# A new order of PE's, ACT's and POOL's instructions in the three-stage front of a decoder block

## The reference, cut to what matters

```python
x = _layernorm(x + _L0_attn_ref(x), axis=-1)          # dilated attention, 16 heads, segments of 64, step 2
x = _layernorm(x + _L0_xattn_ref(x, ctx_512, L0_xattn_Wq, L0_xattn_Wkv_expand, L0_xattn_Wout), axis=-1)
x = _layernorm(x + _L0_ffn_ref(x, L0_ffn_gate_w, L0_ffn_w_gate, L0_ffn_w_up, L0_ffn_w_down), axis=-1)
...
# dilated attention: every head attends, inside a segment, over its 32 rows; q = k = v = x
scores = jnp.einsum('bnhqd,bnhkd->bnhqk', g, g) * scale
out = jnp.einsum('bnhqk,bnhkd->bnhqd', jax.nn.softmax(scores, axis=-1), g)
...
# cross attention: 16 heads of 16 columns, 128 x 128 causal scores per head, keys and values from ctx
scores = jnp.where(causal, jnp.einsum('bhqd,bhkd->bhqk', qh, kh) * inv_sqrt_d, jnp.finfo(scores.dtype).min)
out = jnp.einsum('bhqk,bhkd->bhqd', jax.nn.softmax(scores, axis=-1), vh)
...
# experts: 32, top 8 of a softmax, each expert takes a limited number of rows in order
probs = jax.nn.softmax(x @ gate_w, axis=-1)
w, sel = jax.lax.top_k(probs, K)
...
y = jnp.einsum('eci,eih->ech', jax.nn.silu(g) * u, w_down)
```

## Time and profile before

| | |
|---|---|
| median of 3 runs | 622.9 us (622.82 to 624.33) |
| the profiled execution | 623.45 us, of which the span of the trace is 621.8 us |
| busy over the span | PE 512.0, DVE 367.2, ACT 335.4, POOL 399.8 us |
| front | from 0 to about 299 us; the queues are padded until about 322 us, then the experts |
| granted TensorE clock in the front's steps | 1.00 of full speed, 0.50 in its last step |

### The profile page before, as it was taken

How to read it: one execution, slowest core, us unless ns; L and a number is a source line. 1 busy time by engine, 2 the same in 40 slices (tenths; PEclk the granted TensorE clock), 3 DMA queues, 4 the chain that set the end, 5 groups by cost and what they waited for, 6 DMA issues and landing times.

```text
span 621.8 us, 17381 instructions
## 1 busy us (share of the span) xinstructions
PE 512.0 (82%) x5065; PEld 393.7 (63%) x5066; DVE 367.2 (59%) x1527; ACT 335.4 (54%) x1204; POOL 399.8 (64%) x604
## 2 busy tenths in 40 slices
PE   2888998888888888885119999999999999994994
PEld 2555555555555555542008888888888888883773
DVE  1468787777777787763304555555555555552664
ACT  2266666666666666663005666666666666661112
POOL 6553666666666666556715777777777768774653
PEclk9599999999999999996558999999999999996998
DMA  9999999932222222222785656656655556666994
GB/s 196 281 242 311 343 341 338 337 135 84 74 74 84 74 79 80 77 85 90 260 272 164 183 177 180 185 171 189 188 180 176 179 171 186 186 180 249 427 418 153
DMA packets 82301, 121.30 MB, mean 195 GB/s; under 512 B 13011, under 2 KB 71901, under 8 KB 80224
## 3 DMA queue, kind: packets, MB, share of 16 engines
q1 hardware_dynamic: 64896, 79.51, 42.0%
q0 software_dynamic: 14016, 38.44, 17.4%
q10 hardware_dynamic: 3360, 2.98, 1.5%
HBM read 56.07 MB, written 69.01 MB: 201 GB/s over the span
## 4 chain that ended last, share of the span: by engine, by line
PE 42%; POOL 16%; issue 14%; DVE 12%; DMA 6%; ACT 5%; ACTq 3%; POOLq 1%; SPq 1%; DVEq 0%
PE bank L796 16%; PE bank L812 11%; POOL queues L533 10%; PE bank L788 7%; DMA wall<-results 4%; DVE kP L1048 3%; ACT pr L873 3%; PE bank L806 3%; ACTq L297 2%; POOL rz L498 1%; POOL rz L492 1%; POOL pair_z L569 1%; DVE nmax L1025 1%; PE bank L614 1%; PE bank L604 1%
## 5 line engine op out<-in xcount | busy, mean ns | idle before, releaser
L559 POOL DMA_INDIRECT results<-ys,wcol x152 | 150.2, 988 | 26.2 <-POOL pscrap L548 24.1
L533 POOL DMA_INDIRECT queues<-x,xidx x128 | 128.5, 1004 | 37.2 <-issue 36.3
L796 PE MATMUL bank<-wall,xtT 128*128 x616 | 127.0, 329 | 0.1
L873 ACT ACTIVATE pr<-bank,nmax 128x128 f32<-128x128 f32 x256 | 90.9, 370 | 29.1 <-DVE nmax L1025 29.1
L796 PEld LDWEIGHTS bank<-wall,xtT 128*128 128x128 f32 x616 | 98.5, 194 | 0.5 <-issue 0.5
L966 ACT ACTIVATE ys<-bank,wcol 128x256 f32<-128x256 f32 x152 | 72.1, 474 | 44.5 <-PE bank L812 44.5
L1219 DVE SCALAR_TENSOR_TENSOR tg<-th,bank 128x96 f32<-128x96 f32 x154 | 39.1, 254 | 90.8 <-ACT th L960 90.6
L788 PE MATMUL bank<-ident,xt 128*128 128x128 f32 x310 | 63.4, 286 | 34.2 <-DMA xt<-queues 22.9
L812 PE MATMUL bank<-wall,hT 96*128 x304 | 90.8, 380 | 0.0
L788 PEld LDWEIGHTS bank<-ident,xt 128*128 128x128 f32 x310 | 59.2, 198 | 48.7 <-DMA xt<-queues 23.9
L604 PE MATMUL bank<-kP,qS 128*128 128x512 f32 x128 | 67.1, 606 | 0.0
(11 more groups left out here) (178 smaller groups left out, 879.6 us busy)
## 6 DMA issues: line engine op xcount, KB each, us to landing
xt<-queues SPq DMA_DIRECT2D x162, 160.0 KB, 2.2
results<-zeros SPq DMA_DIRECT2D x16, 1024.0 KB
wall<-results SPq DMA_DIRECT2D x16, 1024.0 KB, 13.9
queues<-zeros SPq DMA_DIRECT2D x32, 160.0 KB, 2.8
wall<-in_L_ffn_w_gate SPq DMA_DIRECT2D x4, 768.0 KB, 11.5
wall<-in_L_ffn_w_up SPq DMA_DIRECT2D x4, 768.0 KB, 13.6
wall<-in_L_ffn_w_down SPq DMA_DIRECT2D x4, 768.0 KB, 13.0
results<-ys,wcol POOLq DMA_INDIRECT x152, 2.6
```

The costliest lines, as they stand in the source:

```text
L533: pool.indirect_dma_start(xg, bass.IndirectOffsetOnAxis(ap=xidx[:, par, k:k + 1], axis=0), x2[:, par, :], None, bounds_check=last_row, oob ...
L559: pool.indirect_dma_start(yr, bass.IndirectOffsetOnAxis(ap=wcol[:, u, 1:2], axis=0), ys[:, u, :], None, bounds_check=last_y, oob_is_err=Fa ...
L796: ins = pe.matmul(bank[2 + u % 2][:, 0:2 * INTER].rearrange("p (g i) -> p g i", g=2), xtT[:, u % 2, kk, :], wall[:, bass.ds(e, GU)].rearrange(
L873: ins = act.activation(pr[:, g % 2, q, :], pS[g % 2][:, q * P:(q + 1) * P], ACT.Exp, bias=nmax[:, 4 * g + q:4 * g + q + 1], accum_out=den[ ...
```

## The change

Three orders are rewritten; no operation is added or removed.

- PE. In step k the dilated matmuls ("o") move ahead of V0, and their wait for "turn" moves into `scores(b, 2)`, between the mask and the scores; S3 moves ahead of V0 and of the transposes of `x2`; T2 moves ahead of V1; the transposes of `x1` move ahead of the keys and values; V2 moves behind the queries; V3 moves ahead of `front`.
- ACT. The exponentials e2 move ahead of the copy of T1; `er` moves ahead of `qS`; the copy of `rT` moves ahead of e0 of the next tile.
- POOL. `root_r` stands ahead of scatter 2 where it stood ahead of scatter 3, and `root_a` ahead of scatter 3 where it stood ahead of scatter 6.

```diff
-        peA = Steps(sem("peA"), "cT s o kv x1T q")
+        peA = Steps(sem("peA"), "cT s o x1T kv q")
-        peB = Steps(sem("peB"), "T0 S2 V0 T1 S3 V1 T2 V2 T3 V3 rT y")
+        peB = Steps(sem("peB"), "T0 S2 T1 S3 V0 T2 V1 V2 T3 V3 rT y")
-        actB = Steps(sem("actB"), "e1 T0 T1 e2 T2 e3 T3 rT")
+        actB = Steps(sem("actB"), "e1 T0 e2 T1 T2 e3 T3 rT")
...
-                        if k == 3 and not (isinstance(r, int) and r == NB - 1):
+                        if k == 2 and not (isinstance(r, int) and r == NB - 1):
                             root_r(r + 3)
-                        if k == 6 and not (isinstance(r, int) and r >= NB - 3):
+                        if k == 3 and not (isinstance(r, int) and r >= NB - 3):
                             root_a(r + 3)
...
-            def scores(b, g, par):
+            def scores(b, g, par, a=None):
...
+                if a is not None:
+                    pe.wait_ge(dveA.sem, dveA.at(a, "turn"))
                 pe.matmul(pS[g % 2][:, :], qS[:, g % 2, m, :], kP[:, par, m, :, :],
...
                     turn_probs(b, 0, None)
-                    scores(b, 2, pb)
-                if a is not None:
-                    pe.wait_ge(dveA.sem, dveA.at(a, "turn"))
-                if b is not None:
-                    if there(b - 1):
-                        pe.wait_ge(dveY.sem, dveY.at(b - 1, "add"))
-                    values(b, 0, pb)
-                if a is not None:
+                    scores(b, 2, pb, a)
+                if a is not None:
+                    if b is None:
+                        pe.wait_ge(dveA.sem, dveA.at(a, "turn"))
                     for j in range(PAIRS):
...
                     turn_probs(b, 1, None)
+                    scores(b, 3, pb)
+                    if there(b - 1):
+                        pe.wait_ge(dveY.sem, dveY.at(b - 1, "add"))
+                    values(b, 0, pb)
...
-                    scores(b, 3, pb)
+                    turn_probs(b, 2, (actB.sem, actB.at(b, "T0")))
                     values(b, 1, pb)
-                    turn_probs(b, 2, (actB.sem, actB.at(b, "T0")))
...
+                    pe.wait_ge(dveN.sem, dveN.at(a, "x1"))
+                    for kk in range(2):
+                        ins = pe.transpose(pX[:, kk * P:(kk + 1) * P], x1[:, par, kk * P:(kk + 1) * P], ident[:, :])
+                    ins.then_inc(peA.sem, 1)
                     pe.wait_ge(actA.sem, actA.at(a, "cT"))
...
-                if a is not None:
-                    pe.wait_ge(dveN.sem, dveN.at(a, "x1"))
-                    for kk in range(2):
-                        ins = pe.transpose(pX[:, kk * P:(kk + 1) * P], x1[:, par, kk * P:(kk + 1) * P], ident[:, :])
-                    ins.then_inc(peA.sem, 1)
-                if b is not None:
-                    values(b, 2, pb)
...
+                if b is not None:
+                    values(b, 2, pb)
                 if r is not None:
                     pe.wait_ge(dveR.sem, dveR.at(r, "pickb"))
...
+                if b is not None:
+                    values(b, 3, pb)
                 if a is not None and not (isinstance(a, int) and a == NB - 1):
                     front(a + 1, 1 - par, r)
-                if b is not None:
-                    values(b, 3, pb)
...
                     probs_T(b, 0)
+                    exps(b, 2)
                     probs_T(b, 1)
-                    exps(b, 2)
...
                     exps(b, 3)
+                if r is not None:
+                    act.wait_ge(dveR.sem, dveR.at(r, "clamp"))
+                    act.activation(er[:, :], lc[:, :], ACT.Exp).then_inc(actR.sem, 1)
                 if a is not None:
                     act.wait_ge(peA.sem, peA.at(a, "q"))
...
-                if a is not None:
-                    exps(a, 0)
                 if b is not None:
                     act.wait_ge(peB.sem, peB.at(b, "rT"))
                     act.copy(flat2(rT[:, :, :]), pO[:, D:2 * D]).then_inc(actB.sem, 1)
+                if a is not None:
+                    exps(a, 0)
```

More of the change, by code:

```diff
@@ L917, in step @@
                     ins.then_inc(actA.sem, 1)
-                if r is not None:
-                    act.wait_ge(dveR.sem, dveR.at(r, "clamp"))
-                    act.activation(er[:, :], lc[:, :], ACT.Exp).then_inc(actR.sem, 1)
                 if a is not None:
```

## The result

The median of four runs is 603.29 us (602.26 to 603.96), that of the kernel before, run on the same chip, 622.86 (622.35 to 624.33). The ratio is 0.968, with a 95% interval of 0.966 to 0.970. The forecast was 604, with a range of 597 to 614.

What follows compares the result with a forecast made beforehand. No engine was taken as the limit, but the order of their waits for each other. 16.6 us in 13 steps, 0 in the head and 2.4 in the tail sum to 19.0, giving 604 us; range 597 to 614.

Steps and rivals of the forecast that it cites:

- the replay: One step worked through in the new order from the end of m0, with old durations and distances: 15.11 us instead of 16.38.
- rT ahead of e0: Head of a step, ACT copying rT before the exponentials: 0.27 us gained of oT's 0.97 wait, bounds 0.1 to 0.5.
- "turn" ahead of S2, "o" ahead of V0: On PE in each step: S2 still gains 0.3 us despite the added wait, and oA comes 0.65 us earlier.
- POOL's roots: On POOL in each step: root_a waits only for ve, so x1 comes 1.47 us earlier, the largest piece.
- The price: Five scatters behind root_a instead of two: keep some 0.8 us late, POOL's round 14.1 us, covered while a step takes more.
- Keys and er: After x1 in each step: keys' copy gains 1.27 us though held by kv; er ready early; keys to m0 3.75 us.
- The round: One whole step closes at 15.11 us, mean 15.2 against 16.48: 1.28 a step, 16.6 us in 13 steps.
- Head and tail: Steps 0 to 2 count 0, with 1 us to both sides; the last steps gain 2.4 us, bounds 0 and 3.05.
- POOL and DVE hold each other up: Shared port pair blocks one DVE instruction a step, 0.29 us in 13 steps, 3.8 us: 608; chance 8%.
- POOL the bound: Each of POOL's 8 scatters takes 0.2 us longer, its round 15.8, and DVE waits at x2: 612; chance 12%.
- The waits come back elsewhere: New waits at S2, the keys and dA take all but 0.3 us of gain a step: 617; chance 7%.
- rT holds e0: Late rT on PE delays e0 on ACT; at 2.0 us behind m0 a step is 0.4 longer: 626; chance 7%.

Runs made afterwards that it cites:

- the fills spread: The changed kernel, with the sixteen 1 MB fills of zeros into the results each waiting for one more tile's keep instead of going at once: 597.43 us.
- the two powers: The changed kernel with two small powers that nothing reads added on POOL behind the eighth scatter of each step: 601.32 us.
- the added matmuls: The changed kernel with fills of zeros spread over the front, plus 80 unread matmuls on PE between the tables and the experts: 595.50 us.

## Why the prediction was right

The time was right, and the large waits go where the replay put them: those of `oT` and `x1` are gone, `dA` waits for `eA`, and POOL waits for `ve` at both roots. Three small waits that it forecast are not there (0.3 of `oA` for PE, 0.1 of `x1` for POOL, 0.2 of the keys for L695), and one that it didn't have is (`x2` for the scatters' landing).

That the sum of 19.0 came out at 19.6 in the medians is in part luck. In the profiles the 13 steps gave 19.2 where I had 16.6, the head 1.1 and the tail 2.4 where I had 0 and 2.4: the front gained 22.8 instead of 19.0. The experts' stretch, which I had taken as fixed, lost 2.6. And the 19.2 are themselves a sum of two errors: shorter rounds, 5.7 more than forecast, and the fills, which take 3.1 of that back.

- *rT ahead of e0.* `dA` waits 0.35 for `eA`, forecast 0.3, and undoing this one step costs 0.22 a step, forecast 0.27. rT on PE starts 0.09 behind the end of m0, and not 0.11 ahead of it: inside the 0.36 that I had allowed.
- *"turn" ahead of S2, "o" ahead of V0.* "o" starts 4.77 behind the end of m0, where the replay has 4.63; `oA` is at 5.85 where it has 6.01. The mis-sized term is the 1.38 from the start of "o" to `oA`: it is 1.08, as the 64 small matmuls took 0.75 us and not the 1.00 of the earlier trace rows, and `oA` follows `x2` on DVE without a wait for PE. Why they are shorter stays open; they take 1.00 in nearly every step of the three profiles with the old order of both PE and ACT, and 0.75 in nearly every step of the other eleven. PE's order as a whole is worth 0.40 a step in the changed kernel.
- *POOL's roots.* Both wait for `ve`, 0.93 and 0.96, forecast over 1 each; `root_a` starts 0.08 behind `ve`'s end, as replayed, and `x1` waits for nothing. `x1` comes 8.41 behind the end of m0, replayed 8.64; the 0.23 is all by which this step is shorter than the replay's 15.11. It is the largest piece, as forecast: without it 17.8 of 19.2 us are gone.
- *The price.* POOL reaches `keep` without idle time, 0.74 behind the end of `xidx`: as forecast. Its round, step less the wait at `root_r`, is 14.88 - 0.93 = 13.95, forecast 14.1. That this lateness is felt by "nobody but the first two scatters" is the sentence that failed: `x2` feels it through the scatters' landing, 2.9 us in three steps, as long as the fills are in the way.
- *Keys and er.* The keys don't wait for kv at all; they come 2.02 behind `x1`, as replayed (2.04), but behind the router's picks on DVE. From the keys to m0 it is 3.76, forecast 3.75.
- *The round* is 14.7 to 14.9 with the fills out of the way, forecast 15.11 to 15.2, and 15.3 to 15.8 in four of the five steps beside the fills; the mean of 15.00 hides the two. With the fills spread 13 rounds take 191.9 us, with the fills in one go 195.0, and 15.2 each would have made 197.6.
- *Head and tail.* The tail gave 2.4, the forecast's number. The head gave 1.1, forecast 0 with 1 to both sides, a little more than its bound; the head goes with the clock, so that this says little of the edits.

The rivals. *POOL and DVE hold each other up* (608): the meeting is there, but off the path. `xidx` takes 0.45 to 0.73 us in seven of its 14 rows from step 2 to step 15, and 0.16 to 0.20 in the others; in the kernel before it takes 0.16 in all 14. In ten of the 14 a scatter is running on POOL when it starts, and in the longest one `gm`. In the step above it is

```profile
149.86 0.46 DVE L1156 TENSOR_SCALAR xidx<-near 128x8 int32<-128x8 f32 x1
```

which ends 0.13 behind the end of the scatter of 149.12. In all ten it ends 0.12 to 0.14 behind, whether the scatter had 0.02 or 0.34 still to run, and 0.04 behind `gm`. But `dA` waits for `eA` anyway. The Trainium skill (SBUF — State Buffer, Terms, shared port pair) has the pair held for a whole instruction and the loser blocked. The trace agrees: `xidx` lost 0.30 us, about the 0.33 that the scatter still had to run; the scatter itself took 1.07 instead of 0.97.

*POOL the bound* (612) is refuted by the two powers. *The waits come back elsewhere* (617) is what each part does alone, and not what the three do together. *rT holds e0* (626) happens at 0.4 us when x1T stands behind kv.

In the 13 steps the three parts give -0.7, -2.6 and 5.8 alone, 2.5 together by addition, and 19.2 in one kernel. Without the two steps at the lower clock (3.3) and the one wait for a scatter (0.9) the addition would give 6.7, still far from 19.2. A single part takes a wait out of a ring in which the next one is already due.

## What to carry to other kernels

Where several engines wait for each other in a ring, replay the whole ring with all edits in it; a part tried alone says little about its worth (POOL's order gave nothing alone and 17.8 us as the last part). When an instruction is made later "at no cost", follow its DMA to the landing and to whoever reuses that buffer, at the traffic of that stretch. Cut both traces at the same events before judging a sum, since a stretch that the edit doesn't touch can move with the clock (the head here by 4 us, the experts by 3).

## What the runs showed of the hardware

- After 23 us with PE idle, the experts start at a clock of 0.50 in all thirteen profiles without the added matmuls. It rises to 1.00 between 4.1 and 11.5 us behind their first transpose; their stretch takes 297.4 to 298.6 us where it rises up to 6.2 us behind, and 299.0 to 300.5 where it rises from 9.5 us on. The Trainium skill (TensorE: Matmul & The Clock Gate, Part 1) says that the point of the rise varies from run to run for one kernel; that is not shown here, since each profile is of another version, but the experts' code is the same in all thirteen and the point varies by 7.4 us.
- The first pair of scores matmuls at about 25 us takes 1.02 us in four profiles and 1.91 to 1.92 in ten, and the head is 55.6 to 55.8 us in those four and 56.6 to 59.7 in those ten.
- The clock can fall inside a busy loop too: in the run of PE's order alone it went to 0.50 in two of 13 steps, and these took 1.6 to 1.7 us longer.
- In the changed kernel an `xidx` on DVE that starts while a scatter runs on POOL ends 0.12 to 0.14 us behind the scatter's end in all ten cases, and takes up to 0.47 us instead of 0.16. A POOL instruction doesn't always hold it: beside the added 128x1 powers, with 0.57 us still to run, it took 0.16.
- Scatters issued from POOL landed 6.8 us after the last had left it while the DMA engines were full (337 GB/s), and held DVE; with 192 GB/s no `x2` waited for them.
